# Gelu once per hidden tile on ScalarE, with the rounded half made by a VectorE copy

## The reference

```python
attn_out = softmax((x@Wq) @ (x@Wk).T * scale) @ (x@Wv) @ Wp + bp
cms_out  = gelu(attn_out @ cW1 + cb1) @ cW2 + cb2 + one_hot(codes)      # 512 -> 2048 -> 512
modifier = gelu(concat([attn_out, cms_out]) @ mW1 + mb1) @ mW2 + mb2    # 1024 -> 2048 -> 512
y   = clip(x + cms_out + modifier, 0, 1)
h   = y + (gelu(y @ W_down[s] + b_down[s]) @ W_up[s] + b_up[s])         # s: one of 3 adapters per sample
out = layernorm(h) * ln_w[s] + ln_b[s]
```

## Time and profile before

| | us |
|---|---|
| timed runs, median of 3 (lowest, highest) | 1170.34 (1169.48, 1170.78) |
| profiled execution | 1170.42 |
| its span, first to last instruction | 1168.6 |
| ScalarE busy | 343.7 (29%) |
| VectorE busy | 624.3 (53%) |
| GpSimd busy | 178.2 (15%) |

### The profile page before, as it was taken

The page is one execution under the profiler, slowest core; times in us unless marked ns, Lnnn a source line. Parts: engine busy times, 40 slices in busy tenths (PEclk is TensorE's granted clock), DMA queues, the critical chain, the costliest instruction groups (busy, mean ns, idle before and its releaser), DMA issues.

```text
span 1168.6 us, 13768 instructions
## 1 busy us (share of the span) xinstructions
PE 1134.7 (97%) x5024; PEld 936.8 (80%) x5024; DVE 624.3 (53%) x930; ACT 343.7 (29%) x599; POOL 178.2 (15%) x120
## 2 busy tenths in 40 slices
PE   7999999999999999999899999999999999999974
PEld 6888887788888888888788888888888888888763
DVE  3734434465665666656944444354444534445968
ACT  3624333322323223224311212122121221213832
POOL 0501102101101101103801111110100111112310
PEclk9999999999999999999999999999999999999988
DMA  7301100100100100100000000000000000001142
GB/s 253 109 1 36 36 1 19 37 19 19 36 18 18 36 18 18 36 19 28 28 27 27 27 27 27 27 2 25 27 27 27 27 27 27 28 31 59 55 126 90
DMA packets 44401, 44.52 MB, mean 38 GB/s; under 512 B 3409, under 2 KB 30033, under 8 KB 44369
## 3 DMA queue, kind: packets, MB, share of 16 engines
q1 hardware_dynamic: 43792, 43.04, 11.4%
q10 hardware_dynamic: 576, 1.05, 0.2%
HBM read 39.88 MB, written 4.19 MB: 38 GB/s over the span
## 4 chain that ended last, share of the span: by engine, by line
PE 91%; DVE 5%; POOL 2%; ACT 1%; DMA 1%; issue 0%; SPq 0%; DVEq 0%; ACTq 0%
PE bank L400 30%; PE bank L402 30%; PE bank L401 30%; DVE stats L904 1%; POOL res L374 1%; DVE z_even L918 1%; PE bank L444 1%; POOL cms_lo L348 1%; DVE res L847 1%; DVE res L834 0%; DVE z_odd L918 0%; DVE z_odd L912 0%; DMA raw<-W_up_dram 0%; DVE z_even L912 0%; POOL wsplit L348 0%
## 5 line engine op out<-in xcount | busy, mean ns | idle before, releaser
L834 DVE TENSOR_TENSOR res<-bank,res 128x512 f32<-128x512 f32 x240 | 163.6, 691 | 259.4 <-PE bank L402 259.3
L643 ACT ACTIVATE gelu_f<-bank,hidden_bias 128x512 f32<-128x512 f32 x128 | 88.3, 690 | 636.0 <-PE bank L402 635.9
L834 DVE TENSOR_TENSOR cms_acc<-bank,cms_acc 128x512 f32<-128x512 f32 x240 | 163.4, 691 | 121.7 <-PE bank L402 121.7
L348 POOL TENSOR_TENSOR wsplit<-raw,wsplit 128x512 fp32r<-128x512 f32 (+1 forms) x64 | 100.8, 1576 | 721.7 <-ACT wsplit L577 721.7
L400 PE MATMUL bank<-attn_hi,wsplit 128*128 128x512 f32 x512 | 199.9, 390 | 3.1 <-DVE cms_lo L841 3.1
L400 PE MATMUL bank<-gelu_hi,wsplit 128*128 128x512 f32 x512 | 199.4, 389 | 1.5 <-DVE gelu_lo L820 1.5
L402 PE MATMUL bank<-attn_hi,wsplit 128*128 128x512 f32 x512 | 199.9, 390 | 0.0
L401 PE MATMUL bank<-attn_lo,wsplit 128*128 128x512 f32 x512 | 199.8, 390 | 0.0
L402 PE MATMUL bank<-gelu_hi,wsplit 128*128 128x512 f32 x512 | 199.2, 389 | 0.0
L401 PE MATMUL bank<-gelu_lo,wsplit 128*128 128x512 f32 x512 | 199.2, 389 | 0.0
L400 PEld LDWEIGHTS bank<-attn_hi,wsplit 128*128 128x128 f32 x512 | 96.6, 189 | 23.6 <-DVE cms_lo L841 3.5
(11 more groups left out here) (112 smaller groups left out, 1187.9 us busy)
## 6 DMA issues: line engine op xcount, KB each, us to landing
raw<-cW_dram SPq DMA_DIRECT2D x32, 256.0 KB, 2.8
raw<-mW_dram SPq DMA_DIRECT2D x16, 512.0 KB, 4.2
res<-xT_dram SPq DMA_DIRECT2D x4, 1024.0 KB, 8.4
x_raw<-x_dram SPq DMA_DIRECT2D x4, 1024.0 KB, 6.1
raw<-mW_dram SPq DMA_DIRECT2D x16, 256.0 KB, 4.3
raw<-W_down_dram SPq DMA_DIRECT2D x4, 512.0 KB, 3.7
raw<-W_up_dram SPq DMA_DIRECT2D x4, 512.0 KB, 4.6
out_dram<-z_even SPq DMA_DIRECT2D x8, 256.0 KB, 2.0
```

The source lines that it names most:

```text
L348: pool.tensor_tensor(dst, src, f32(hi), ALU.subtract).then_inc(done, 1)
L643: act.activation(dst[:, g, :], bank[r][:, :], ACT.Gelu, bias=hidden_bias[:, s:s + 1]).then_inc(gelu_made, 1)
L834: op = dve.tensor_tensor(dst, src, dst, ALU.add)
```

## The change

ScalarE evaluates the Gelu once per unit, into `gelu_f`. VectorE copies `gelu_f` into `gelu_hi`, which rounds it, waits on a new semaphore `gelu_hi_made` for its own copy, and subtracts as before. `gelu_made` now counts 1 per unit up to unit 127 and 2 per adapter tile as before, so the waits on it are rewritten. ScalarE no longer waits for the output tiles of unit i-2, since it does not write `gelu_hi` any more.

```diff
+        gelu_hi_made = sem("gelu_hi_made")
...
-                    pe.wait_ge(gelu_made, 2 * (UNITS + i - 3))
+                    pe.wait_ge(gelu_made, UNITS + (1 if i < 3 else 2) * (i - 3))
...
                     act.wait_ge(gelu_lo_made, i - 1)
-                    act.wait_ge(out_filled, i * 4 - 4)
-                for dst in (gelu_f, gelu_hi):
-                    act.activation(dst[:, g, :], bank[r][:, :], ACT.Gelu, bias=hidden_bias[:, s:s + 1]).then_inc(gelu_made, 1)
+                act.activation(gelu_f[:, g, :], bank[r][:, :], ACT.Gelu, bias=hidden_bias[:, s:s + 1]).then_inc(gelu_made, 1)
...
             def gelu_lo_unit(i, g):
-                dve.wait_ge(gelu_made, i * 2 + 2)
+                dve.wait_ge(gelu_made, i + 1)
+                dve.tensor_copy(gelu_hi[:, g, :], gelu_f[:, g, :]).then_inc(gelu_hi_made, 1)
+                dve.wait_ge(gelu_hi_made, i + 1)
                 dve.tensor_tensor(gelu_lo[:, g, :], gelu_f[:, g, :], f32(gelu_hi[:, g, :]), ALU.subtract).then_inc(gelu_lo_made, 1)
...
-                    dve.wait_ge(gelu_made, 2 * (UNITS + BT * b + m + 1))
+                    dve.wait_ge(gelu_made, UNITS + 2 * (BT * b + m + 1))
```

## The result

| | before | changed |
|---|---|---|
| median of 17 timed runs, us | 1170.39 | 1173.70 |
| lowest, highest, us | 1169.48, 1171.27 | 1171.30, 1176.23 |
| ratio of the changed to before, 95% interval | | 1.0029 (1.0022 to 1.0035) |
| profiled execution, us (span) | 1170.42 (1168.6) | 1176.23 (1174.4) |

The change costs 3.3 us, 0.29%, which is more than the 0.2% that a measurement of this kernel can tell. It also widens the scatter: the 17 times fall into three groups, five from 1171.3 to 1172.2, seven from 1173.3 to 1174.1 and five from 1175.4 to 1176.2.

A forecast was written before the change was run, and what follows sets the result against it. The prediction took TensorE, busy 97% of the span, as the bound, with VectorE the bound in the transition between the MLPs. Start -0.1, transition +1.9 and end 0 gave +1.8 us: 1172.1 us, range 1170.2 to 1174.0.

The forecast's parts named there:

- the forecast's own band: Whole kernel: a loss of +0.8 to +2.3 us, a little above the 0.2% line in part; chance 0.60.
- the first of the slower rivals: Units 61 to 66 and last two units: one more GpSimd turn, 3.0 plus 0.7 us, 1174.0; chance 0.18.
- The copy's duration, 0.42 us plus 0.04 and 0.08: Each unit's VectorE chain: copy 0.42, semaphore wait 0.04, lost overlap 0.08; 0.5 us added, 0.8 at the upper bound.
- The long loops, nothing: First and modifier MLP loops: no loss, as TensorE's cover of 1.0 and 3.7 us absorbs the copy.
- Start, -0.1: First serial Gelu chain: 0.58 us goes out, 0.46 comes in, so -0.1 us.
- End, 0: End of the modifier MLP, near 1086 us: counted 0, with ends of -0.3 and +0.7 us.
- Unit 61 and 62, stalls of 0.85 and 1.4: Transition between the MLPs: copy and subtraction queue behind GpSimd turns, stalling TensorE 0.85 us, then 1.4 more.
- `cms_lo` of sample 0 done +2.1 late, TensorE again idle for 3.1: Transition: four residue subtractions done at 566.1, +2.1 us; TensorE's 564.03 becomes 566.1 after 3.1 us idle.
- The same counting with two more copies puts its end at 583.9, +1.8 on TensorE: Transition, third cms_lo group: end moves from 581.04 to 583.9, making TensorE 1.8 us later.
- So 1.8 to 2.1 either way: Transition: loss 1.8 to 2.1 us whether or not the 1.7 us clock drop repeats; 1.9 taken, ends 0.5 and 3.0.

The follow-up runs named there:

- the first experiment: Changed kernel, but in units 61 to 65 ScalarE evaluates the Gelu twice as before: 1169.12 us against 1169.94 for the kernel before.
- the order experiments: GpSimd's adds for samples 1 to 3 held until VectorE finished the previous sample's cms_lo: changed kernel 1169.51 us, kernel before 1165.96, against 1169.94.
- the second experiment: Kernel before, with VectorE's copy replacing the second Gelu in units 61 to 65 only: 1173.38 us against 1169.94 for the kernel before.

## Why the prediction came out as it did

The measured 1173.7 lies inside the range of 1170.2 to 1174.0, 1.6 us above the predicted 1172.1, and the loss of 3.3 us lies above the forecast's own band (+0.8 to +2.3). The likelier side was given to "within 0.2%" (0.64) and it came out slower by more than that (0.33). What happened is the first of the slower rivals (0.18), by its mechanism, one GpSimd turn more, but at another place than it named. That the median lies inside the range is in part luck: six of the 17 single times are above 1174.0, and nothing in the prediction says that the times fall into groups or how often each comes.

- *The copy's duration, 0.42 us plus 0.04 and 0.08*: right. 419 ns, and 0.47 us more on the chain against 0.5.
- *The long loops, nothing*: right; no wait of TensorE between 224 and 545 us, and the first experiment shows that all copies outside units 61 to 65 together cost nothing that can be measured.
- *Start, -0.1*: TensorE's wait went from 0.77 to 0.65 us. *End, 0*: its wait near 1086 went from 0.72 to 0.61, and the first experiment bounds both ends together.
- *Unit 61 and 62, stalls of 0.85 and 1.4*: right. The idle column counts from the end of the matmul in front, so the loss is better read from starts. The last matmul in front of the first wait started at 552.52, so with the usual 0.23 between starts the next was due at 552.75 and came at 553.56: 0.81. After 24 more (5.44 us, and 0.11 since the first one took 0.50 in place of 0.39) the second was due at 559.11 and came at 560.29: 1.18, against a forecast of 1.4. The working writes 1.2 us for a turn of GpSimd, but its own times (551.7 to 552.7) take 1.0, which is what the turn took: the copy ends at 551.81 and the subtraction, 0.69 long when alone, at 553.51.
- *`cms_lo` of sample 0 done +2.1 late, TensorE again idle for 3.1*: from the due time of unit 61's output tiles to the start of unit 64 it was 11.43 us before (552.60 to 564.03) and is 13.20 now (552.75 to 565.95): +1.8, with an idle time of 2.6. The sizes are off by 0.3 and 0.5, the order of the turns is the one counted.
- *"The same counting with two more copies puts its end at 583.9, +1.8 on TensorE"*: this is the step that failed. I followed the four adds of sample 3 and left out what stands behind them on GpSimd's list, the split of block 33. At unit 66 TensorE was 3.3 us late in the first profile (585.54 - 552.75 against 582.08 - 552.60). In the execution of the lowest group, where the split came too late to be in front, it was 1.8 late (582.75 against a due time of 551.49), and with the split held back 1.2 (583.23 against 552.57; both due times are the end of the first wait, 552.30 and 553.38, less the same 0.81). That the 1.8 equals the forecast is luck: it is the lateness of unit 64 carried on, behind which the clock falls as in the kernel before, and TensorE does not wait for `cms_lo` at unit 66. Where VectorE's turns do set the time, as the forecast had it, with the split held and the clock at full, it is 1.2. So the missed term is 1.5 to 2.1 us, and by their times 12 of the 17 runs have it. Part of this step is a term that the prediction left out here without a reason: it moved ScalarE's cast 0.58 earlier at the first loop and at the end, and not in the transition, where the split was ahead by 0.46. Times are compared from the due times because single executions differ before the change can act: in the five profiles of the changed kernel the first wait ends between 552.30 and 553.56.
- *"So 1.8 to 2.1 either way"*, on the clock: wrong as well. I had seen that a clock that stays up makes TensorE early, and held that VectorE then bounds it at the same time. In fact an early TensorE sets off the split earlier, and that costs more than the clock gives: the lower clock behind unit 64's start, 1.7 us of work by itself (granted 0.99 in 561 to 566 us and 0.67 in 566 to 571), belongs to the quickest executions.

**The rule on the shared pair.** VectorE and GpSimd alternate: the copies of units 61 to 64 last 0.97 to 1.32 us in place of 0.42 and the subtractions about 1.66 in place of 0.69, whereas the adds between them, with one input in PSUM, keep their 0.69 beside a busy GpSimd:

```profile
554.57 2.74 DVE L835 TENSOR_TENSOR cms_acc<-bank,cms_acc 128x512 f32<-128x512 f32 x4 [1.06 <-PE bank L403]
...
557.22 1.32 DVE L819 CAST gelu_hi<-gelu_f 128x512 fp32r<-128x512 f32 x1
...
558.58 1.65 DVE L821 TENSOR_TENSOR gelu_lo<-gelu_f,gelu_hi 128x512 fp32r<-128x512 f32 x1
...
554.61 2.40 POOL L349 TENSOR_TENSOR wsplit<-raw,wsplit 128x1024 fp32r<-128x1024 f32 x1
```

The Trainium skill (SBUF — State Buffer, section "SBUF: two separate sides") says that a VectorE operation in a 2-port mode, or one with two SBUF inputs, and a GpSimd operation that reads SBUF exclude each other for the whole instruction. All these rows agree with it, and the order experiments agree with its consequence: delays go by whole instructions.

## What to carry to other kernels

Splitting one VectorE instruction into two on a chain shared with GpSimd can cost a whole GpSimd instruction on top of the copy's own time, since the second half has to queue again; count turns, and count them down the whole of GpSimd's list. An engine's relief is worth nothing where it waits for the bottleneck (here 73 us of ScalarE). Follow the relieved engine too: what it does earlier may start work elsewhere that gets in the way (here an estimate, not a test). And when two engines take turns, look whether the order can be fixed by a wait: here two waits gave 5.4 us to the unchanged kernel.

## What the hardware showed that I had not expected

A lower TensorE clock can go with a quicker kernel: the profiled execution with the lower clock behind unit 64's start took 1171.5 us and the four without it 1173.8 to 1176.2, and the second experiment's profile, with the lower clock there too, took 1171.1. The same idle time in front of unit 64, 2.65 us, was followed by the lower clock in the execution of 1171.53 us and not in those of 1173.76 and 1175.63; nothing here shows what decides it. And the times of one kernel can scatter in steps: 4.9 us between the lowest and the highest of 17 runs, where the kernel before has 1.8, from one race between VectorE and GpSimd and the clock around it.
